# Second attention of a fused layer: scores from three bf16 parts packed by DMA, rotation partner by DMA, batches unrolled and overlapped

## The chip, the cores and the metric

The kernel runs on one core of a Trainium2 chip. The metric is the device time of one execution in microseconds (us). The engines are TensorE (PE; its weight loads are listed as PEld), VectorE (DVE), ScalarE (ACT), GpSimd (POOL) and SyncE (SP), which issues DMAs.

## The reference

A layer over x of 8 batches x 256 positions x 512 features: a first attention whose output feeds the second, the second attention (below), a GRU over the 256 positions and a mixture of 8 experts with top 2. Only the second attention is touched:

```python
q, k, v = (proj(Wq), proj(Wk), proj(Wv))          # 16 heads of 32
q, k = _rope(q, k, s, d, hidden_states.dtype)     # q*cos + rotate_half(q)*sin
scores = jnp.einsum('bhqd,bhkd->bhqk', q, k) / math.sqrt(d)
scores = jnp.maximum(scores + causal, neg)
tmp_attn = jax.nn.softmax(scores.astype(jnp.float32), axis=-1)
tmp_sum = jnp.sum(tmp_attn, axis=-2)
_, topk_idx = jax.lax.top_k(tmp_sum, heavy_budget)       # 25 of 256 columns
heavy_mask = jnp.any(topk_idx[..., :, None] == jnp.arange(s), axis=-2)
band = jnp.abs(i - j) <= recent_budget
scores = jnp.where(heavy_mask[:, :, None, :] | band, scores, neg)
probs = jax.nn.softmax(scores.astype(jnp.float32), axis=-1)
attn = jnp.einsum('bhqk,bhkd->bhqd', probs, v)
return attn @ Wo.T
```

The choice of the 25 columns must come out as in fp32, which is why scores are made in fp32 or from parts that add up to it.

## The kernel before

`program` runs the first attention (its output hT stands in SBUF by 45 us), then `second_attention`, then the GRU and the experts together, which take the rest. Every engine has a program of its own; they are ordered by semaphores alone, and each engine does its instructions in the order written.

`second_attention` goes over the 8 batches in a hardware loop (`Fori`), one batch after another, with two rounds over 16 heads in each. The 512 features are four tiles (KD) of 128, a tile is four heads of 32 rows.

- Projections (`project`, L479) for the next batch: q and k transposed, fp32, 32 matmuls of 256 columns into banks 0 to 3. They run between the rounds, while VectorE chooses columns. ScalarE copies them to `raw` (L612).
- Rotation: `swap` (L490) brings each row's partner with a permutation matmul from the table; VectorE multiplies by sine (L688), by cosine (L691) and adds (L693), 1024 columns each, for q and then k, at the end of a batch. k is then copied four times with the rows of the other heads at zero (`kz`, ScalarE L619 and VectorE L697), so that a score matmul can contract over all 128 rows.
- Round one, `scores(b, 0, h)`: two bf16 matmuls put the causal mask in a bank (L460, L461), then fp32 scores, 128 query rows x 128 columns (L469) and 128 x 256 (L471). Bank is h % 4, so head h waits for the exponentials of head h - 4 (`a_e`). VectorE takes two maxima (L669, L670), ScalarE exponentials with sums (L602, L604), VectorE the reciprocals (L676) into `rdiag` (L707), and for four heads at a time TensorE sums columns (L516). A `v` projection (L505, 8 matmuls of 512 columns, from the copy `hb` that GpSimd makes, L428) precedes the last sums.
- VectorE chooses the 25 largest columns for the 16 heads at once (L717 to L733), TensorE transposes the result (L526), VectorE copies it (L736), GpSimd makes a diagonal matrix for each head (L421).
- Round two, `scores(b, 1, h)`: as before with three more bf16 matmuls by the diagonals (L466 to L468); then normalised (L747, L749), transposed three heads behind (L544), copied (L638), attended in fours (L560, L563), copied to `oT` (L643, L645). At the batch's end the output projection (L575) into banks 0 to 3, and VectorE adds it to `x1T` (L757). The next batch's first score waits for the first add (`v_x`).

Of the kernel before, what the change touches and what calls it, by code (L numbers as in the profile page):

```python
# [13 lines left out]
P = 128  # L14
# [27 lines left out]
C_ROT = 0  # L42
C_CAUS = C_ROT + P
# [312 lines left out]
def second_attention(nc, ps, cst, ident, x1T, hT, tab, weights, d_w, d_tab, d_xT, sb, sem):  # L356
    st = ExitStack()
    with st:
        wq, wk, wv, wo = weights
        masks = sb(st, "masks", [P, 4, P], BF16)  # L360
        hb = sb(st, "hb", [P, KD, S])
        raw = sb(st, "raw", [P, 2, KD, S])
        rot = sb(st, "rot", [P, 2, KD, S])
        kz = sb(st, "kz", [P, HPC, KD, S])
        v = sb(st, "v", [P, KS, D])
        tmp = sb(st, "tmp", [P, KD, S])
# [18 lines left out]
        c_hb = sem(st, "c_hb")  # L385
        p_qk = sem(st, "p_qk")
        a_raw = sem(st, "a_raw")
        p_rot = sem(st, "p_rot")
        v_rot = sem(st, "v_rot")
        a_kz = sem(st, "a_kz")  # L390
        v_kz = sem(st, "v_kz")
# [19 lines left out]

        with nc.Block() as block:
            @block.gpsimd
            def _(pool):
                def diagonals(b):

                    pool.wait_ge(v_l, b + 1)
                    for h in range(NH):
                        if h >= NDG:
                            pool.wait_ge(p_s, b * 2 * NH + NH + h - NDG + 2)  # L420
# [5 lines left out]
                with pool.Fori(0, B) as b:  # L426
                    pool.wait_ge(p_v, b + 1)
                    nc.gpsimd.tensor_copy(hb[:, :, :], hT[:, :, bass.ds(b, 1), :].rearrange("p k a s -> p k (a s)"))\  # L428
                        .then_inc(c_hb, 1)
                    diagonals(b)  # L430

            @block.tensor
            def _(pe):

                pe.nop().then_inc(p_v, 1)
                pe.nop().then_inc(p_s, 1)
# [4 lines left out]
                def scores(b, r, h, more=False):  # L441
# [4 lines left out]
                    if r == 0 and h < 4:  # L446
                        if h == 0:
                            pe.wait_ge(v_x, b * KD + 1)
                    else:
                        pe.wait_ge(a_e, (n - 4 + 1) * 2)  # L450
                    if r == 0 and h == 0:
                        pe.wait_ge(v_rot, b * 6 + 6)
                    if r == 0 and h < 2:
                        pe.wait_ge(a_kz, b * 2 + h + 2)
                    elif r == 0 and h < HPC:
                        pe.wait_ge(v_kz, b * 2 + h - 1)
                    if r == 1 and h == 0 and more:
                        pe.wait_ge(a_raw, b * 2 + 4)
# [3 lines left out]
                    if r == 1:  # L462
# [11 lines left out]
                def project(b):  # L474

                    for i, w in enumerate((wq, wk)):
                        for m in range(KD):
                            for k in range(KD):
                                last = nc.tensor.matmul(ps[:, 2 * i + m // 2, (m % 2) * S:(m % 2 + 1) * S],  # L479
                                                        w[:, k, m * P:(m + 1) * P],  # L480
                                                        hT[:, k, bass.ds(b, 1), :].rearrange("p a s -> p (a s)"),
                                                        start=(k == 0 and m % 2 == 0), stop=(k == KD - 1),
                                                        skip_group_check=True)
                        last.then_inc(p_qk, 1)

                def swap(b, i):

                    pe.wait_ge(a_raw, b * 2 + i + 1)
                    for m in range(KD):
                        last = nc.tensor.matmul(ps[:, 4 + 2 * i + m // 2, (m % 2) * S:(m % 2 + 1) * S],  # L490
                                                tab[:, C_ROT:C_ROT + P], raw[:, i, m, :],
                                                start=(m % 2 == 0), stop=True, skip_group_check=True)
                    last.then_inc(p_rot, 1)

                def batch(b, more):

                    for h in range(NH + AHEAD_SUMS):
                        if h < NH:
                            scores(b, 0, h)
                        if h == NH:  # L500

                            pe.wait_ge(c_hb, b + 1)
                            for c in range(KS):
                                for k in range(KD):
                                    last = nc.tensor.matmul(ps[:, 6 + c, :], hb[:, k, c * P:(c + 1) * P], wv[:, k, :],  # L505
                                                            start=(k == 0), stop=(k == KD - 1))
                            last.then_inc(p_v, 1)
                        g = h - AHEAD_SUMS
                        if g >= 0 and g % CGS == CGS - 1:

                            g0 = g - CGS + 1
# [18 lines left out]
                    for h in range(NH + AHEAD + 1):  # L530
                        if h < NH:
                            scores(b, 1, h, more)
# [1108 lines left out]
```

## Time and profile before

| | us |
|---|---|
| median of 3 runs (lowest to highest) | 2241.44 (2241.01 to 2247.59) |
| the profiled execution | 2239.64 |
| its span, first to last instruction | 2237.8 |
| mean granted TensorE clock | 0.947 |
| busy PE / PEld / DVE / ACT / POOL | 2033.8 / 1748.2 / 1325.7 / 950.0 / 230.7 |

A line of the page's table of slices is a share of busy time in tenths for 40 slices of 56 us; the second attention is slices 1 to 13. A timeline row is start, duration, engine, line, operation, output<-input, shape and count; what stands in brackets is the idle time before it and what ended it. PE durations include the pipeline, so that what a matmul costs is read from start to start.

### The profile page before, as it was taken

How to read it: one execution, taken by the hardware profiler on the slowest of the kernel's cores; microseconds unless marked ns; L12 is line 12 of the kernel's file. 1: busy time of each engine (PE TensorE's matmuls, PEld its weight loads, DVE VectorE, ACT ScalarE, POOL GpSimd, SP SyncE). 2: the span in 40 equal slices, each digit the busy share in tenths (PEclk: the TensorE clock that was granted, in tenths of full speed). 3: DMA queues.
4: the chain of work that ended last, by engine and by line, in shares of the span. 5: the costliest groups of instructions: out<-in, count | busy, mean ns of one | idle time of the engine just before them, and what ended most of it. 6: DMA issues, size and time to landing. Idle time of an engine off the chain costs nothing.

```text
span 2237.8 us, 86088 instructions
## 1 busy us (share of the span) xinstructions
PE 2033.8 (91%) x34733; PEld 1748.2 (78%) x34733; DVE 1325.7 (59%) x4942; ACT 950.0 (42%) x3354; POOL 230.7 (10%) x346
## 2 busy tenths in 40 slices
PE   5889999999996889766999999998999989999999
PEld 3677677767665768666898998898998988988987
DVE  3565575575565079555666666665666656666653
ACT  1355364464453212233444444443444444444432
POOL 0011011011102100000011010110110110111012
PEclk9999999999997999865899999999999999999999
DMA  6000000000000832200000000000000000000000
GB/s 249 1 1 0 0 0 0 0 0 0 0 1 32 291 113 73 67 17 3 18 17 18 13 18 18 27 4 19 27 4 28 18 19 13 18 18 13 4 12 10
DMA packets 53629, 66.07 MB, mean 30 GB/s; under 512 B 4384, under 2 KB 45792, under 8 KB 52416
## 3 DMA queue, kind: packets, MB, share of 16 engines
q1 hardware_dynamic: 50832, 46.48, 6.2%
q0 software_dynamic: 2448, 14.68, 2.0%
q8 instruction: 250, 4.10, 0.8%
q14 instruction: 99, 0.81, 0.1%
HBM read 44.34 MB, written 16.81 MB: 27 GB/s over the span
## 4 chain that ended last, share of the span: by engine, by line
PE 51%; DVE 4%; issue 2%; ACT 1%; DMA 0%; DVEq 0%; POOL 0%; ACTq 0%
PE ps L1302 27%; PE ps L1256 11%; PE ps L1236 11%; PE ps L1290 2%; PE ps L1245 1%; DVE hbuf L1472 1%; DVE dh L1460 0%; DVE dh L1466 0%; DVE hbuf L1469 0%; DVE cn L1450 0%; DVE ns L1462 0%; DVE h L1470 0%; ACT nn L1369 0%; DVE s L1438 0%; DVE cn L1438 0%
## 5 line engine op out<-in xcount | busy, mean ns | idle before, releaser
L1302 PE MATMUL ps<-hbuf,whf 128*128 128x32 f16 x24480 | 659.1, 178 | 82.9 <-DVE hbuf L1472 59.9
L1302 PEld LDWEIGHTS ps<-hbuf,whf 128*128 128x128 f16 x24480 | 648.3, 97 | 106.0 <-DVE hbuf L1472 60.4
L1349 ACT ACTIVATE rz<-s,sc 128x32 f32<-128x32 f32 x512 | 164.5, 321 | 524.1 <-DVE s L1438 512.6
L1236 PE MATMUL ps<-hbuf,w1f 128*128 128x256 f16 x2304 | 294.4, 275 | 0.0
L1256 PE MATMUL ps<-hh,w2f 128*128 128x256 f16 x2304 | 294.1, 276 | 0.0
L1438 DVE TENSOR_REDUCE s<-ps 128x32 f32<-128x64 f32 x512 | 114.5, 224 | 272.7 <-PE ps L1302 259.4
L1425 POOL TENSOR_TENSOR hh<-tb,hh 128x256 f16<-128x256 f32 x192 | 132.3, 694 | 1307.2 <-ACT hh L1396 1307.2
L1236 PEld LDWEIGHTS ps<-hbuf,w1f 128*128 128x128 f16 x2304 | 224.5, 98 | 33.3 <-issue 6.0
L1256 PEld LDWEIGHTS ps<-hh,w2f 128*128 128x128 f16 x2304 | 212.0, 98 | 45.9 <-issue 19.6
L946 PE MATMUL ps<-x1T,wi 128*128 x768 | 173.7, 389 | 21.2 <-DMA wi<-in_W_ih 12.6
L946 PEld LDWEIGHTS ps<-x1T,wi 128*128 128x128 f32 x768 | 149.1, 195 | 45.4 <-issue 19.6
L471 PE MATMUL ps<-kz,rot 128*128 128x256 f32 x512 | 160.2, 396 | 0.0
L1341 ACT ACTIVATE ps<-gi,sc 128x64 f32<-128x64 f32 x512 | 152.7, 298 | 13.8 <-issue 9.9
L1438 DVE TENSOR_REDUCE cn<-ps 128x32 f32<-128x64 f32 x256 | 57.4, 224 | 138.5 <-PE ps L1302 138.5
L421 POOL TENSOR_TENSOR dg<-masks,lcol 128x256 bf16<-128x256 bf16 x128 | 78.2, 616 | 568.7 <-DVE lcol L736 490.9
L602 ACT ACTIVATE E<-ps,nm 128x128 f32<-128x128 f32 x256 | 94.2, 368 | 85.9 <-DVE nm L670 83.0
L1386 ACT ACTIVATE sg<-ps,b,sc 128x256 f32<-128x256 f32 x192 | 105.1, 548 | 48.1 <-PE ps L1236 48.1
L604 ACT ACTIVATE E<-ps,nm 128x256 f32<-128x256 f32 x256 | 119.9, 468 | 0.0
L1534 DVE SCALAR_TENSOR_TENSOR tb<-ps,b1s,sg 128x256 f32<-128x256 f32 x192 | 92.1, 480 | 43.5 <-ACT sg L1386 42.2
L469 PE MATMUL ps<-kz,rot 128*128 128x128 f32 x512 | 117.6, 313 | 0.0
L972 ACT ACTIVATE stage<-ps,bsum 128x256 f32<-128x256 f32 x96 | 44.8, 473 | 167.0 <-PE ps L946 141.0
L669 DVE TENSOR_REDUCE nm<-ps 128x1 f32<-128x128 f32 x256 | 73.7, 288 | 55.6 <-PE ps L471 55.2
(198 smaller groups left out, 2876.3 us busy)
## 6 DMA issues: line engine op xcount, KB each, us to landing
gi_d<-stage SPq DMA_DIRECT2D x96, 128.0 KB, 1.7
gi<-gi_d SPq DMA_DIRECT2D x16, 768.0 KB, 5.5
w1f<-in_w1T POOLq DMA_DIRECT2D x4, 1408.0 KB, 9.2
xall<-in_x SPq DMA_DIRECT2D x4, 1024.0 KB, 9.0
x1T<-in_xT SPq DMA_DIRECT2D x1, 4096.0 KB, 21.7
w2f<-in_w2T POOLq DMA_DIRECT2D x2, 2048.0 KB, 11.0
out<-x1T SPq DMA_DIRECT2D x8, 512.0 KB, 3.1
wi<-in_W_ih SPq DMA_DIRECT2D x1, 3072.0 KB, 10.5
```

The source lines that it names most:

```text
L469: nc.tensor.matmul(ps[:, bank, 0:P], rot[:, 0, m, 0:P], kz[:, q, m, 0:P], start=False, stop=True, skip_group_check=True)
L471: nc.tensor.matmul(ps[:, bank, P:P + S], rot[:, 0, m, P:S], kz[:, q, m, :], start=False, stop=True, skip_group_check=True).then_inc(p_s, 1)
L604: nc.scalar.activation(E[:, h % NEX, P:P + S], ps[:, bank, P:P + S], ACT.Exp, bias=nm[:, r, h, 1:2], accum_out=ls[:, r, h, 1:2]).then_inc( ...
L946: last = nc.tensor.matmul(ps[:, q % 4, 0:TT], wi[:, k, q * P:(q + 1) * P], x1T[:, k, bass.ds(t * SPT, SPT), :].rearrange("p s b -> p (s b) ...
L1236: last = nc.tensor.matmul(ps[:, 6 + i % 2, 0:TT], w[:, wp, e % EH, c * P:(c + 1) * P], hbuf[par][:, k, hq, :, :].rearrange("p s b -> p (s ...
L1256: last = nc.tensor.matmul(ps[:, 4 + m // 2, (m % 2) * TT:(m % 2 + 1) * TT], w[:, wp, e % EH, m * P:(m + 1) * P], hh[:, i % RING, hq, :], s ...
L1302: last = nc.tensor.matmul(ps[:, bank, g * WIDE * 2 * B:(g + 1) * WIDE * 2 * B], whp[:, k, w, q, g * P:(g + 1) * P], h[:, k, :, :].unsqueez ...
L1341: return nc.scalar.activation(of_bank(bank), of.unsqueeze(2).broadcast_to((P, KD, 2, B)), ACT.Copy, scale=sc[:, S_G2:S_G2 + 1])
L1349: nc.scalar.activation(rz[:, q, :, :].rearrange("p g b -> p (g b)"), s1[:, q, :, :].rearrange("p g b -> p (g b)"), ACT.Sigmoid, scale=sc[: ...
L1386: nc.scalar.activation(sg[:, i % 2, :], ps[:, 6 + i % 2, 0:TT], ACT.Sigmoid, bias=b1[:, c, e:e + 1], scale=sc[:, S_UN1:S_UN1 + 1]).then_in ...
L1425: nc.gpsimd.tensor_tensor(hh[:, i % RING, 1, :], tb[:, i % TB, :], hh[:, i % RING, 0, :], ALU.subtract).then_inc(g_l, 1)
L1438: nc.vector.tensor_reduce(o, of_bank(bank).rearrange("p g a b -> p g b a"), AX.X, ALU.add)\
```

## The change

All of it is in `second_attention` and its table.

1. Scores. After rotation, GpSimd splits q and k into three bf16 parts (`split`: high part, remainder, middle part, low part; four operations on 512 columns for each of four units). SP stores the parts to DRAM (`store`) and loads them back (`pack`), for each head three parts under one another on 96 partitions, in two "ways" (`SLOTS`). A score is then two accumulating bf16 matmuls in place of one fp32, giving the six products that matter. `kz` and its copies go.
2. The rotation partner: eight DMAs from SBUF to SBUF for each unit, each 16 partitions x 2 KB, take the place of the permutation matmuls.
3. A unit is q or k for two of the four feature tiles (`UNITS`). Projection (8 parts), raw copies (4), rotation (12 steps of 512 columns) for the next batch stand in round one at given heads, as does the rest of the batch before (last three transposes, last attend, output projection, adds).
4. The values are projected from hT directly in two halves around the last column sums; `hb` goes. Batches are unrolled in Python; there are four diagonals in flight instead of three.

Core of the diff (the first "for b in range(B)" is SP's program, the second TensorE's, the third VectorE's round one):

```diff
+NU = 4
+UNITS = ((0, 0), (1, 0), (0, 1), (1, 1))
+UNIT_BANK = (6, 6, 7, 6)
+PROJECT_AT = (0, 1, 3, 4, 6, 7, 8, 10)
+RAW_AT = (2, 5, 8, 11)
+ROTATE_AT = (4, 5, 6, 7, 8, 9, 10, 11, 12, 13, 14, 15)
+CLOSE_AT = (12, 13)
+ADD_AT = (14, 15)
+SLOTS = (((0, 0, 1), (1, 0, 2)), ((0, 1, 0), (1, 2, 0)))
+            @block.sync
+                def swap(b, u):
+                    i, p = UNITS[u]
+                    sp.wait_ge(a_raw, b * NU + u + 1)
+                    passed(sp, v_rot, (b * NU + u - 1) * 3)
+                    half = DH2 // 2
+                    for to in range(0, P, half):
+                        of = to + half if to % DH2 == 0 else to - half
+                        sp.dma_start(swp[to:to + half, u % 2, :, :], raw[of:of + half, i, 2 * p:2 * p + 2, :])\
+                            .then_inc(d_swap[u % 2], 16)
+                def store(b, u):
+                    sp.wait_ge(g_part, (b * NU + u + 1) * 4)
...
+                    for j in range(3):
+                        sp.dma_start(parts_d[i, j][:, p * 2 * S:(p + 1) * 2 * S],
+                                     parts[:, i, j, 2 * p:2 * p + 2, :].rearrange("p m s -> p (m s)"))\
+                            .then_inc(d_parts[u], 16)
+                def pack(b, p):
+                    for u in (2 * p, 2 * p + 1):
+                        sp.wait_ge(d_parts[u], (b + 1) * 3 * 16)
+                    if b:
+                        sp.wait_ge(p_s, b * 2 * NH - NH + (p + 1) * NH // 2)
+                    for i in range(2):
+                        for way in range(2):
+                            for slot, j in enumerate(SLOTS[i][way]):
+                                of = parts_d[i, j].rearrange("(q d) n -> d q n", d=DH2)
+                                sp.dma_start(pk[slot * DH2:(slot + 1) * DH2, i, way, :, 2 * p:2 * p + 2, :]
+                                             .rearrange("d q m s -> d q (m s)"),
+                                             of[:, :, p * 2 * S:(p + 1) * 2 * S]).then_inc(d_pack[p], 16)
+                for b in range(B):
+                    swap(b, 0)
+                    swap(b, 1)
+                    store(b, 0)
+                    swap(b, 2)
+                    store(b, 1)
+                    swap(b, 3)
+                    store(b, 2)
+                    store(b, 3)
+                    for p in range(2):
+                        pack(b, p)
+                def split(b, u):
...
+                    x = raw[:, i, 2 * p:2 * p + 2, :]
...
+                    nc.gpsimd.tensor_copy(part[0], x).then_inc(g_part, 1)
+                    nc.gpsimd.tensor_tensor(x, x, part[0], ALU.subtract).then_inc(g_part, 1)
+                    nc.gpsimd.tensor_copy(part[1], x).then_inc(g_part, 1)
+                    nc.gpsimd.tensor_tensor(part[2], x, part[1], ALU.subtract).then_inc(g_part, 1)
+                    if r == 0 and h % (NH // 2) == 0:
+                        pe.wait_ge(d_pack[h // (NH // 2)], (b + 1) * PACK)
-                    nc.tensor.matmul(ps[:, bank, 0:P], rot[:, 0, m, 0:P], kz[:, q, m, 0:P],
-                                     start=False, stop=True, skip_group_check=True)
-                    nc.tensor.matmul(ps[:, bank, P:P + S], rot[:, 0, m, P:S], kz[:, q, m, :],
-                                     start=False, stop=True, skip_group_check=True).then_inc(p_s, 1)
+                    for way in range(2):
+                        nc.tensor.matmul(ps[:, bank, 0:P], pk[:, 0, way, q, m, 0:P], pk[:, 1, way, q, m, 0:P],
+                                         start=False, stop=(way == 1), skip_group_check=True)
+                    for way in range(2):
+                        last = nc.tensor.matmul(ps[:, bank, P:P + S], pk[:, 0, way, q, m, P:S],
+                                                pk[:, 1, way, q, m, :],
+                                                start=False, stop=(way == 1), skip_group_check=True)
...
+                for b in range(B):
+                    for h in range(NH):
+                        scores(b, 0, h)
+                        if b and h < AHEAD:
+                            turn(b - 1, NH - AHEAD + h)
+                        if b and h == AHEAD:
+                            attend(b - 1, KD - 1)
+                        if b < B - 1 and h in PROJECT_AT:
+                            u, part = divmod(PROJECT_AT.index(h), 2)
+                            if part == 0:
+                                if u == 0:
+                                    passed(pe, a_o, (b - 1) * KD + KD - 1)
...
+                                if u % 2 == 1:
+                                    pe.wait_ge(a_raw, (b + 1) * NU + u // 2 + 1)
+                            project(b + 1, u, part, UNIT_BANK[u])
+                        if b and h in CLOSE_AT:
+                            m = CLOSE_AT.index(h)
+                            close(b - 1, m, 5)
+                        if h >= AHEAD_SUMS and (h - AHEAD_SUMS) % CGS == CGS - 1:
...
+                            column_sums(b, (h - AHEAD_SUMS) // CGS)
...
+                    values(b, 0)
+                    column_sums(b, NH // CGS - 1)
+                    values(b, 1)
+                    if b:
+                        pe.wait_ge(v_x, (b - 1) * KD + 2)
+                        close(b - 1, 2, 5)
+                        close(b - 1, 3, 5)
...
+                def rotate(b, u, step):
...
+                    x, y = raw[:, i, 2 * p:2 * p + 2, :], swp[:, u % 2, :, :]
...
+                    if step == 0:
+                        dve.wait_ge(d_swap[u % 2], (b * 2 + u // 2 + 1) * 8 * 16)
+                        nc.vector.tensor_tensor(y, y, sin, ALU.mult).then_inc(v_rot, 1)
+                    if step == 1:
+                        nc.vector.tensor_tensor(x, x, cos, ALU.mult).then_inc(v_rot, 1)
+                    if step == 2:
+                        dve.wait_ge(v_rot, n + 2)
+                        nc.vector.tensor_tensor(x, x, y, ALU.add).then_inc(v_rot, 1)
...
+                for b in range(B):
+                    for h in range(NH):
+                        maxima(b, 0, h)
...
+                            for_sums(b, h - 1)
+                        if b < B - 1 and h in ROTATE_AT:
+                            u, step = divmod(ROTATE_AT.index(h), 3)
+                            rotate(b + 1, u, step)
+                        if b and h in ADD_AT:
...
+                            add(b - 1, ADD_AT.index(h), 5)
-NDG = 3
+NDG = 4
```

ScalarE's program for round one is: `exps(b, 0, h)`, at heads 0 and 1 the last two copies of transposes of the batch before, at head 4 its last `oT` copy, and after the exponentials of heads 2, 5, 8 and 11 a raw copy of 512 columns. In round two VectorE adds the last two parts of the batch before at heads 0 and 1.

## Rows read from the trace of the kernel before

**Rows 1.** One row each of the source views of L717 and L757, all batches.

```profile
L717 DVE COPY tsum<-ps x8: 424/424/425, 100.7 to 670.4; 128x256 f32<-128x256 f32 x8
...
L757 DVE TENSOR_TENSOR x1T<-ps,x1T x32: 595/612/629, 154.5 to 719.4; 128x256 f32 x28, 128x256 f32<-128x256 f32 x4
```

**Rows 2.** Windows: length, busy PE, PEld, DVE, ACT, POOL, then PEclk, DMA share, GB/s.

```profile
197.46:225.35 27.89, 25.68 (x257) 20.64 (x257) 20.43 (x80) 21.36 (x83) 10.62 (x17) 1.00 0.00 0
...
74.36:79.60 5.24, 5.24 (x21) 4.14 (x22) 1.92 (x9) 2.81 (x9) 0.00 (x0) 0.50 0.00 0
```

**Rows 3.** Timeline: start, us, engine, line; TensorE, a head of round one.

```profile
244.45 0.22 PE L460 MATMUL ps<-masks 128*128 128x128 bf16 x1
...
244.56 0.44 PE L469 MATMUL ps<-kz,rot 128*128 128x128 f32 x2
244.83 0.60 PE L471 MATMUL ps<-kz,rot 128*128 128x256 f32 x2
245.27 0.22 PE L460 MATMUL ps<-masks 128*128 128x128 bf16 x1
```

**Rows 4.** Timeline: VectorE, a head of round two.

```profile
205.77 0.28 DVE L669 TENSOR_REDUCE nm<-ps 128x1 f32<-128x128 f32 x1
...
205.97 0.41 DVE L670 TENSOR_REDUCE nm<-ps 128x1 f32<-128x256 f32 x1
...
207.09 0.28 DVE L669 TENSOR_REDUCE nm<-ps 128x1 f32<-128x128 f32 x1
```

**Rows 5.** Timeline: ScalarE, a head of round two.

```profile
206.41 0.37 ACT L602 ACTIVATE E<-ps,nm 128x128 f32<-128x128 f32 x1
...
207.22 0.49 ACT L638 ACTIVATE ET<-ps 128x384 f32<-128x384 f32 x1
```

**Rows 6.** Timeline: TensorE and VectorE in the middle of a batch.

```profile
174.52 7.03 PE L505 MATMUL ps<-wv,hb 128*128 128x512 f32 x16
181.48 0.86 PE L516 MATMUL ps<-E,rdiag 128*32 128x128 f32 x16
...
196.18 0.61 PE L526 MATMUL ps<-cst,light 128*128 128x128 f32 x4
...
196.83 0.42 DVE L736 COPY lcol<-ps 128x256 f32<-128x256 f32 x1 [7.73 <-PE ps L526]
...
198.00 0.23 PE L466 MATMUL ps<-dg,masks 128*128 128x128 bf16 x1 [0.26 <-POOL dg L421]
```

**Rows 7.** Timeline: TensorE at the tail of a batch.

```profile
228.91 7.07 PE L575 MATMUL ps<-oT,wo 128*128 128x256 f32 x32
238.66 0.23 PE L460 MATMUL ps<-masks 128*128 128x128 bf16 x1 [2.69 <-DVE x1T L757]
```

**Rows 8.** Timeline: DMA issues of SyncE.

```profile
8.06 0.32 SPq L145 DMA_DIRECT2D scr_bias<-bias  x1
8.42 0.31 SPq L146 DMA_DIRECT2D scr_ksc<-ksc  x1
...
729.19 1.29 SPq L925 DMA_DIRECT2D b<-in_b1T  x3
```

**Rows 9.** DMA view: issues, KB each, median us to landing.

```profile
bgi<-in_b_ih SPq DMA_DIRECT2D x1, 6.0 KB, 1.7
```

**Rows 10.** Groups by line in 0 to 800 us: busy us, mean ns.

```profile
L688 DVE TENSOR_TENSOR tmp<-ps,tab 128x1024 f32<-128x1024 f32 x16 | 19.6, 1225 | 50.8 <-PE ps L490 31.5 <-issue 18.4
...
L421 POOL TENSOR_TENSOR dg<-masks,lcol 128x256 bf16<-128x256 bf16 x128 | 78.2, 616 | 568.7 <-DVE lcol L736 490.9 <-PE ps L471 77.6
```

**Rows 11.** Timeline: a GpSimd copy and a VectorE multiply beside it.

```profile
216.56 1.04 POOL L428 COPY hb<-hT 128x1024 f32 x1
...
216.78 0.89 DVE L747 TENSOR_SCALAR En<-E,rl 128x128 f32<-128x128 f32 x1
```

**Rows 12.** Timeline: TensorE at the first score, and the last output projection.

```profile
74.36 0.29 PE L460 MATMUL ps<-masks 128*128 128x128 bf16 x1 [6.88 <-ACT kz L619]
...
709.92 9.46 PE L575 MATMUL ps<-oT,wo 128*128 128x256 f32 x32 [0.53 <-ACT oT L645]
```

More of the change, by code:

```diff
@@ L424, in diagonals @@
                             .then_inc(g_d, 1)
[L426 to L429, printed above, removed]
+                for u in range(NU):
+                    split(0, u)
+                for b in range(B):
+                    if b < B - 1:
+                        for u in range(NU):
+                            split(b + 1, u)
                     diagonals(b)
@@ L486, in swap @@
[L486 to L511, printed above, removed]
-                            pe.wait_ge(v_d, b * NH + g + 1)
-                            for part, (e0, e1) in enumerate(((0, P), (P, P + S))):
-                                for g in range(g0, g0 + CGS):
-                                    rows = (g % CGS) * CG
-                                    last = nc.tensor.matmul(ps[rows:rows + CG, 4, 0:e1 - e0], rdiag[:, g, part, :],
-                                                            E[:, g % NEX, e0:e1], start=(g0 == 0 and part == 0),
-                                                            stop=(g0 + CGS == NH and part == 1),
-                                                            tile_position=(0, rows), skip_group_check=True)
-                            last.then_inc(p_c, 1)
-                    if more:
-                        pe.wait_ge(a_e, (b * 2 * NH + NH) * 2)
-                        project(b + 1)
-                    pe.wait_ge(v_k, b * K_STEPS + K_STEPS)
@@ new lines, in scores, with project @@
+                    last.then_inc(p_s, 1)
+                def project(b, u, part, bank):
+                    i, p = UNITS[u]
+                    w = (wq, wk)[i]
+                    m = 2 * p + part
+                    for k in range(KD):
+                        last = nc.tensor.matmul(ps[:, bank, part * S:(part + 1) * S], w[:, k, m * P:(m + 1) * P],
+                                                hT[:, k, b, :], start=(k == 0 and part == 0), stop=(k == KD - 1),
+                                                skip_group_check=True)
+                    if part == 1:
+                        last.then_inc(p_qk, 1)
@@ new lines, in close @@
+                def close(b, m, bank):
+                    pe.wait_ge(a_o, (b + 1) * KD)
+                    o = ps[:, bank, (m % 2) * S:(m % 2 + 1) * S]
+                    for k in range(KD):
+                        last = nc.tensor.matmul(o, wo[:, k, m * P:(m + 1) * P], oT[:, k, :],
+                                                start=(k == 0 and m % 2 == 0), stop=(k == KD - 1),
+                                                skip_group_check=True)
+                    last.then_inc(p_o, 1)
@@ L579, in _ @@
-                project(0)
-                for i in range(2):
-                    swap(0, i)
-                with pe.Fori(0, B - 1) as b:
-                    batch(b, True)
-                batch(B - 1, False)
+                            attend(b, g // HPC)
+                for g in range(NH - AHEAD, NH):
+                    turn(B - 1, g)
+                attend(B - 1, KD - 1)
+                for m in range(KD):
+                    close(B - 1, m, 2 * (m // 2))
             @block.scalar
@@ L652, in _ @@
+                for g in range(NH - 2, NH):
+                    turned(B - 1, g)
+                attended(B - 1, KD - 1)
             @block.vector
```

346 lines of the change are left out of this document (168 added, 178 removed).

## Prediction, made before the changed kernel was run

> **What bounds the kernel now.** I read the source view first, to bound the part that is changed: the eight column sums are copied out at a pitch of (670.4 - 100.7) / 7 = 81.4 us, so this is a batch's period, and the last add to x1T starts at 719.4 and ends at 720.0 [rows 1]. The second attention is thus 720.0 - 45 of the 2237.8 us; nothing behind it is touched. Then the timeline of one batch, where the reader looks for who is late at each step:
> - Round one, 17.5 us: a head costs TensorE 0.11 for two mask matmuls, 0.27 for fp32 scores on 128 columns and 0.44 on 256 columns, 0.82 in all [rows 3].
> - The middle: values 174.52 to 181.48, column sums 0.8, projections of the next batch until 196.18, then the transpose of the chosen columns, and the first diagonal matmul of round two at 198.00 [rows 6]. VectorE had its choice ready at 196.83 - 7.73 = 189.1: it waits for TensorE.
> - Round two, 27.9 us to the end of the last attend: TensorE is busy for 25.68, but DVE for 20.43 and ACT for 21.36 too [rows 2], and both run without a gap at 1.32 a head [rows 4, 5]. Three engines are nearly level, so a cheaper TensorE frees little here.
> - The tail: swap matmuls, the output projection from 228.91, 7.07, rotation and x1T adds on DVE, until TensorE resumes at 238.66 after 2.69 idle [rows 7].
>
> **The change part by part.** I cost a period of the new loop in three stretches, each by the engine that ends it.
>
> *Scores.* Four bf16 matmuls take the place of the two fp32. Masks at 0.057 for 128 columns [rows 3] are the nearest rows; 2 x 0.057 + 2 x 0.115 = 0.34 against 0.71, so 0.37 off a head. If K=96 tiles with fresh weights load slower, the bound is no gain. Round two's TensorE head falls from 1.32 to 0.95, and DVE with ACT become its bound.
>
> *Round two, from its first diagonal matmul.* First maxima 1.1 later, maxima 0.6, fifteen further heads at 1.30 (I take 1.30 of the 1.32 [rows 4], as POOL and TensorE get out of the way little), two adds of 0.6 moved into it [rows 1], and then ACT: exponentials of head 15 at 0.81 [rows 5], one turned copy 0.49, one oT copy 0.38 and a release. 1.1 + 0.6 + 19.5 + 1.2 + 1.9 = 24.3. There the next batch's first projection part may start, since it waits on that oT copy. The pack DMAs of heads 0 to 7 are issued at head 7: 12 issues at 0.45 and 1.7 to land, some 7 to 10 us with 1.5 MB to move, against 11 us or more; cost zero, hidden by the second half of round two, and up to 5 if that cover is gone.
>
> *Round one.* TensorE's work from here: 15 scores x 0.46 = 6.9, eight projection parts x 1.77 = 14.1 (16 matmuls took 7.07 [rows 7]), two output parts 3.5, three column sums 2.4, turns and one attend 1.5: 28.3, and the first half of the values 3.5: 31.8 until the last column sums. DVE's work is smaller (about 23). But the rotation partner is now a transfer in the middle of DVE's program. Four times DVE reaches the multiply by sine (heads 4, 7, 10, 13) and waits for eight DMAs, and the maxima of all later heads are queued behind that wait; ACT's exponentials, and behind them the next raw copy, wait for those maxima. The loop from the end of one such multiply to the next wait's end is:
> - DVE maxima of the next head 0.62, release 0.07;
> - ACT exponentials 0.81 [rows 5] and raw copy of 512 columns 0.6 (0.49 for 384 [rows 5]): 1.41, release 0.1;
> - SP: eight issues. Two DMAs of 8 rows x 2 KB started 0.36 apart [rows 8]; three others took 0.43 each [rows 8]. I take 0.38, so the last starts 2.66 after the first;
> - landing 1.7 [rows 9], plus 0.1.
>
> That is 6.7, plus the multiply on 512 columns, 0.65 (1225 for 1024 [rows 10]): 7.3 for three heads, where DVE's own work would be 4.5 and TensorE's 5.4. Bounds on the swap itself: 3.5 to 6.
>
> *POOL and DVE.* A split is two copies and two two-input operations: 2 x 0.55 (1.04 for 1024 columns [rows 11]) + 2 x 1.2 (616 ns for 256 [rows 10]) + waits = 3.9. It begins after the third rotation step, so it ends about when the next partner lands. A DVE instruction that met a POOL copy took 0.89 where its like took 0.29 [rows 11]: I add 0.5 for each of three units, between 0 and 1.2. The Trainium skill (SBUF — State Buffer, Who interferes with whom) says that a DVE operation with two SBUF inputs is shut out for the whole of a GpSimd instruction that reads SBUF; with a full 1.2 for each unit the time would be 2230, an estimate by that page. The row shows only the one-input form, and agrees that far.
>
> So round one: first swap landed at 11.6 after the start of the first projection part (4.3 of projections and scores, 2.8 of maxima, exponentials and copy, 4.5 of swap), 0.65, three loops 3 x (7.3 + 0.5) = 23.4, then heads 14 and 15 with steps and adds 4.8: 40.5. TensorE's 31.8 is hidden below it. The Trainium skill (DMA: Bandwidth & Descriptors, Anatomy of one DMA) gives about 2.0 us fixed for a DMA, where [rows 9] show 1.7; by the page's figure, an estimate, the time would be 2223.
>
> *Middle.* Column sums 0.8; then values' second half and two output parts, 3.5 + 3.5 = 7.1, against DVE's choice of 189.1 - 181.5 = 7.6 with the sums in it: level. But TensorE has by then sat idle for some 5 us. After 6.88 idle [rows 12] its granted clock was 0.50, the 1.2 GHz level, for 5.24 us [rows 2], and one output projection took 9.46 [rows 12] where the other took 7.07 [rows 7]; 2.4 more, between 0 and 4. Transpose at 196.18 to diagonal matmul at 198.00: 1.8 [rows 6]. Sum 12.1.
>
> *Period:* 24.3 + 40.5 + 12.1 = 76.9 against 81.4.
>
> *Start.* Before, the first score starts at 74.36 [rows 12]. Now SP's queue serialises the start: unit 0 is projected at about 53.6, copied, swapped, rotated and split by 65; the swap of unit 2 stands on SP behind the store of unit 0, that of unit 3 behind the store of unit 1, and the packs behind the last store. 65 + store 1.3 + swap of unit 2 and store of unit 1 5 + swap of unit 3 4.5 + rotation 2 + split 3.9 + store 1.3 + pack 8 = 91: 17 later.
>
> *Last batch* has no projections and no swap: DVE 16.5 to the sums, middle 9.7, round two 24.3, then three copies and the last attend 3.1, output projection 9.46 cold and an add 0.6: 63.7. In the first batch round one is 2.9 longer: a first score of 0.5, and 2.4 for the clock of a start after idle.
>
> *End* = 91 + 79.8 + 6 x 76.9 + 63.7 = 695.9, against 720.0: 24 us sooner. The profiled execution took 2239.6 with a span of 2237.8; 2239.6 - 24 = 2215. Its median of runs is 2 us higher, which is inside the error.
>
> **The rivals.**
> - *The partner lands in time.* If the swap takes under 2.8 us or DVE gets ahead, round one ends with TensorE at 31.8, TensorE is never idle (middle 9.7), the period is 65.8: seven times 11.1 less, 2137. For it: each transfer is only 32 KB. Against: eight issues of 0.36 by rows of this trace are 2.5 before any landing. 0.20.
> - *POOL's split is long, and slower than before.* SP stores unit 0 before it may swap unit 2, and unit 1 before unit 3. With a split of 3.9 the store is done about 1 us before the swap could be issued. If fp32 doubles the price of two-input operations (the row is bf16 alone), a split is 7: two swaps are late by 2.2 each and the rotations meet POOL's lock for 2 more, 6.4 a batch, 2260. It decides from 3.4 a batch, a split of about 5.5. 0.17.
> - *The scores don't get cheaper*: the bf16 matmuls are as slow as fp32. TensorE stays level with DVE in round two and under the swap waits in round one: 1 us a batch, 2222. 0.05.
>
> **How the numbers follow.** Forecast 0.58, its own range 2190 to 2240 (swap 3.5 to 6 would be -28 to +42 for all units, cold clock -17 to +11, seldom together). To leave out 2 in 10 the range takes in the first rival and half of the second: 2135 to 2255. A change of 0.3%, 7 us, is what a measurement can tell. Faster 0.76 (most of forecast, first and third rival), within 0.08, slower 0.16.
>
> **What would show it.** DVE idle before the sine multiply, released by the swap DMA, about 2 to 4 us, four times a batch; period 77; TensorE idle some 5 us before the last column sums and slow scores or values behind it; first score near 91; round two at 1.3 a head with TensorE idle in it; bf16 score matmuls 57 and 115 ns apart. What makes it wrong: a swap much shorter or longer than 4.5, a late pack (TensorE waiting at head 0 for DMA), or TensorE still full in round two.

## The result: slower by 0.6%, and the profile after

The changed kernel takes 2255.64 us (median of 7 runs, 2250.0 to 2261.17) against 2241.44; the ratio is 1.0056, with a 95% interval of 1.0041 to 1.0072. The forecast was 2215, range 2135 to 2255, faster. The direction was wrong. The profiled execution took 2250.0, the shortest of the seven, with a span of 2248.2. Its page (engine busy times; granted clock in 40 slices; waits for DMA do not show here):

```profile
span 2248.2 us, 85076 instructions
...
PE 1935.9 (86%) x34605; PEld 1655.0 (74%) x34605; DVE 1309.5 (58%) x4974; ACT 927.3 (41%) x3362; POOL 336.4 (15%) x466
...
PEclk9689989989989899956899999999999999999999
```

TensorE is busy 98 us less than before and the span is 10.4 us longer. Source views of the copy of the column sums, one a batch, and of the x1T adds, answering [rows 1]:

```profile
L831 DVE COPY tsum<-ps x8: 424/425/426, 145.0 to 690.5; 128x256 f32<-128x256 f32 x8
...
L800 DVE TENSOR_TENSOR x1T<-ps,x1T x32: 606/616/626, 220.7 to 733.3; 128x256 f32<-128x256 f32 x32
```

The last add ends at 733.9 where it ended at 720.0. The pitch, (690.5 - 145.0) / 7 = 77.9, has the short last batch in it; over the six full batches between the first column sums (144.1) and the seventh (634.3) it is 81.7. Four of the longest waits of the stretch with the second attention in it (us in total, times, longest):

```profile
ACT E L688 <- DVE nm L756: 277.6, 101, 35.0
DVE swp L775 <- DMA swp<-raw: 153.2, 32, 12.6
...
PE ps L561 <- DVE rdiag L794: 79.5, 22, 6.3
...
PE ps L518 <- DMA pk<-parts_d: 33.9, 1, 33.9
```

VectorE waits 153 us for `swp<-raw`, four times in each of 8 batches. Batch 1 to 2 in the new kernel, TensorE, from the first projection part to the last column sums, then to the first diagonal matmul, then to the next batch's first projection part:

```profile
177.24 1.99 PE L542 MATMUL ps<-hT,wq 128*128 128x256 f32 x8 [1.28 <-ACT oT L713]
...
212.68 1.51 PE L561 MATMUL ps<-E,rdiag 128*32 128x128 f32 x16 [4.20 <-DVE rdiag L794]
...
223.58 0.86 PE L561 MATMUL ps<-E,rdiag 128*32 128x128 f32 x16 [3.71 <-DVE rdiag L794]
...
233.06 0.61 PE L654 MATMUL ps<-cst,light 128*128 128x128 f32 x4
...
234.88 0.23 PE L524 MATMUL ps<-dg,masks 128*128 128x128 bf16 x1 [1.10 <-POOL dg L489]
...
258.64 1.99 PE L542 MATMUL ps<-hT,wq 128*128 128x256 f32 x8 [1.28 <-ACT oT L713]
```

That is 46.3 + 11.3 + 23.8 = 81.4 a batch. The middle is 5.2 shorter than before (16.5, [rows 6]) and the old tail of 13.3 is gone [rows 2, 7], but all that and more went into round one. TensorE waits 4.20 and 3.71 for VectorE before its last two column sums.

Answering [rows 3] and [rows 4], a bf16 pair of score matmuls in round one and two maxima of successive heads of round two:

```profile
186.33 0.28 PE L528 MATMUL ps<-pk 96*128 96x128 bf16 x2
186.44 0.38 PE L531 MATMUL ps<-pk 96*128 96x256 bf16 x2
...
242.78 0.29 DVE L755 TENSOR_REDUCE nm<-ps 128x1 f32<-128x128 f32 x1
...
243.97 0.28 DVE L755 TENSOR_REDUCE nm<-ps 128x1 f32<-128x128 f32 x1
```

The bf16 scores came as priced: 0.11 us for two of 128 columns. Where nothing holds it, round two runs at 1.19 us a head on VectorE, not 1.32; over the fifteen steps of this round two, from the first maxima at 235.59 to the last at 257.07, it is 1.35 without the two adds. TensorE's saving is real; it ends in waits.

### The profile page after: what moved, and what is told of

Read it like the earlier page. It is cut to its first block, busy times and chain, and to the rows that moved or that the text cites. A ratio compares the mean times of both kernels' runs of the same rounds, so it can differ in the third digit from the quotient of the medians.

```text
span 2248.2 us, 85076 instructions
## 1 busy us (share of the span) xinstructions
PE 1935.9 (86%) x34605; PEld 1655.0 (74%) x34605; DVE 1309.5 (58%) x4974; ACT 927.3 (41%) x3362; POOL 336.4 (15%) x466
## 4 chain that ended last, share of the span: by engine, by line
PE 50%; DVE 4%; issue 2%; ACT 1%; DMA 0%; DVEq 0%; POOL 0%; ACTq 0%
PE ps L1415 27%; PE ps L1369 11%; PE ps L1349 10%; PE ps L1403 2%; PE ps L1358 1%; DVE hbuf L1585 1%; DVE dh L1573 1%; DVE dh L1579 1%; DVE cn L1563 0%; DVE hbuf L1582 0%; ACT nn L1482 0%; DVE h L1583 0%; DVE cn L1551 0%; DVE ns L1575 0%; DVE hn L1566 0%
## 5 line engine op out<-in xcount | busy, mean ns | idle before, releaser
L775 DVE TENSOR_TENSOR swp<-swp,tab 128x512 f32<-128x512 f32 x32 | 22.9, 715 | 153.2 <-DMA swp<-raw 153.2
L756 DVE TENSOR_REDUCE nm<-ps 128x1 f32<-128x256 f32 x256 | 106.0, 414 | 0.0
L531 PE MATMUL ps<-pk 96*128 96x256 bf16 x512 | 103.4, 285 | 0.0
```

The costliest lines, as they stand in the source:

```text
L531: last = nc.tensor.matmul(ps[:, bank, P:P + S], pk[:, 0, way, q, m, P:S], pk[:, 1, way, q, m, :], start=False, stop=(way == 1), skip_group ...
L756: nc.vector.tensor_reduce(nm[:, r, h, 1:2], ps[:, bank, P:P + S], AX.X, ALU.max, negate=True).then_inc(v_m, 1)
```

## The ring in round one

A ring is a chain of waits that closes on itself: here VectorE waits for a transfer, and the next transfer can only be requested after work that stands behind this wait. VectorE's sine multiplies of batch 2's units, with the idle time before each and what ended it, and one turn of the ring from ScalarE's exponentials over the raw copy to SP's eight DMAs:

```profile
190.69 0.69 DVE L775 TENSOR_TENSOR swp<-swp,tab 128x512 f32<-128x512 f32 x1 [2.93 <-DMA swp<-raw]
...
200.73 0.69 DVE L775 TENSOR_TENSOR swp<-swp,tab 128x512 f32<-128x512 f32 x1 [5.74 <-DMA swp<-raw]
...
209.73 0.69 DVE L775 TENSOR_TENSOR swp<-swp,tab 128x512 f32<-128x512 f32 x1 [4.70 <-DMA swp<-raw]
...
218.72 0.69 DVE L775 TENSOR_TENSOR swp<-swp,tab 128x512 f32<-128x512 f32 x1 [4.70 <-DMA swp<-raw]
...
201.99 0.37 ACT L688 ACTIVATE E<-ps,nm 128x128 f32<-128x128 f32 x1 [6.32 <-DVE nm L756]
...
202.80 0.59 ACT L698 ACTIVATE raw<-ps 128x512 f32<-128x512 f32 x1
...
203.41 4.94 SPq L426 DMA_DIRECT2D swp<-raw  x8
```

From 200.73: exponentials start 1.26 later, raw copy 0.81 behind that, its end at 203.39, SP issues from 203.41 for 4.94, and the last of the eight lands 1.38 later, when the next multiply starts at 209.73. 1.26 + 0.81 + 0.59 + 0.02 + 4.94 + 1.38 = 9.0. Eight DMAs of 32 KB take SP 0.62 us each, where the prediction took 0.38 with 0.43 as the dear end of its rows [rows 8].

The turn before it, from 190.69 to 200.73, takes 10.0, and SP's row for its eight DMAs shows where:

```profile
193.37 5.96 SPq L426 DMA_DIRECT2D swp<-raw  x8
```

One of these eight took SP 1.61 where the others took 0.51 to 0.59. In each batch one turn is longer than 9.0 in this way (9.4 to 10.2). Why a single issue is so long now and then stays open.

Theory A: this ring, and in it the number of issues, sets round one. Rivals: the landing or the bytes (B), the order of the engines' programs whatever brings the partner (C), TensorE after all (D), GpSimd's splits, or the unrolled instruction stream (G). All ratios below are to the kernel before.

## Experiments

**One DMA for the partner.** It leaves out the exchange of rows and moves the same bytes; VectorE's wait, not shown in the cut, then counts one DMA.

```diff
-                    for to in range(0, P, half):
-                        of = to + half if to % DH2 == 0 else to - half
-                        sp.dma_start(swp[to:to + half, u % 2, :, :], raw[of:of + half, i, 2 * p:2 * p + 2, :])\
-                            .then_inc(d_swap[u % 2], 16)
+                    sp.dma_start(swp[:, u % 2, :, :], raw[:, i, 2 * p:2 * p + 2, :]).then_inc(d_swap[u % 2], 16)
```

> Leaves out the exchange of rows: the partner is copied by one DMA of 128 partitions x 2 KB in place of eight of 16 partitions, so each unit still crosses the same bytes and the same wait, with one issue. Theory A (the eight issues, 4.94 us on SP in the changed kernel, make the loop of 9.0 us between sine multiplies): the loop shortens by the seven issues of 0.62, 9.0 - 4.3 = 4.7 us, which is near VectorE's own work for three heads, so round one falls to what TensorE needs: a batch shorter by 10 to 14 us, the whole by 75 to 110 us. Rival B (the wait is the landing of a DMA and the lock that GpSimd's split holds, not the count): the loop stays above 8 us and the whole moves by less than 20 us.

Measured 2160.56 us, ratio to before 0.9637 (0.9609 to 0.9665), 95 us below the changed kernel. VectorE's sine multiplies, then SP's single issue:

```profile
173.39 0.68 DVE L771 TENSOR_TENSOR swp<-swp,tab 128x512 f32<-128x512 f32 x1
...
179.49 0.98 DVE L771 TENSOR_TENSOR swp<-swp,tab 128x512 f32<-128x512 f32 x1 [0.67 <-DMA swp<-raw]
...
185.85 0.79 DVE L771 TENSOR_TENSOR swp<-swp,tab 128x512 f32<-128x512 f32 x1 [0.86 <-DMA swp<-raw]
...
177.22 0.47 SPq L423 DMA_DIRECT2D swp<-raw  x1
```

In this batch they are 6.1 to 6.4 apart and the wait is gone or under 1 us; in others single turns take up to 7.6. The ring alone had expected 4.7; by then TensorE is the one without a gap, busy in the whole 6.10 from 173.39 to 179.49. Same bytes, an eighth of the issues: A, against B.

**Four DMAs**, again without the exchange of rows and with VectorE's wait to match:

```diff
-                    for to in range(0, P, half):
-                        of = to + half if to % DH2 == 0 else to - half
-                        sp.dma_start(swp[to:to + half, u % 2, :, :], raw[of:of + half, i, 2 * p:2 * p + 2, :])\
+                    for to in range(0, P, DH2):
+                        sp.dma_start(swp[to:to + DH2, u % 2, :, :], raw[to:to + DH2, i, 2 * p:2 * p + 2, :])\
```

> Leaves out the exchange of rows: the partner is copied by four DMAs of 32 partitions in place of eight of 16, the same bytes. Between the changed kernel (eight, sine multiplies 9.0 us apart) and the run with one DMA (6.1 to 6.4 apart, where VectorE and TensorE set the pace). Theory A, the price is per issue, 0.62 us on SP: 9.0 - 4 x 0.62 = 6.5 us apart, so nearly the whole gain of one DMA: 2170 to 2190 us. Rival B, the price is per byte or per row: four DMAs take SP about as long as eight, and the time stays above 2230 us.

Measured 2189.06 us, ratio 0.9767 (0.9748 to 0.9787). Sine multiplies and SP:

```profile
175.81 0.69 DVE L773 TENSOR_TENSOR swp<-swp,tab 128x512 f32<-128x512 f32 x1 [0.44 <-DMA swp<-raw]
...
182.55 1.35 DVE L773 TENSOR_TENSOR swp<-swp,tab 128x512 f32<-128x512 f32 x1 [1.09 <-DMA swp<-raw]
...
189.93 1.13 DVE L773 TENSOR_TENSOR swp<-swp,tab 128x512 f32<-128x512 f32 x1 [2.43 <-DMA swp<-raw]
...
196.88 1.35 DVE L773 TENSOR_TENSOR swp<-swp,tab 128x512 f32<-128x512 f32 x1 [2.21 <-DMA swp<-raw]
...
193.06 2.41 SPq L424 DMA_DIRECT2D swp<-raw  x4
...
182.20 1.16 POOL L479 TENSOR_TENSOR parts<-raw,parts 128x512 bf16<-128x512 f32 x1
```

Four DMAs of twice the size take SP 2.41, 0.60 each. The price is per issue. The multiplies are 6.7 to 7.4 apart, not 6.5, because three of the four shown take 1.13 to 1.35 instead of 0.69: now that the partner lands earlier, the multiply meets GpSimd's split, the lock that the prediction had put into the slower ring. The multiply at 182.55 starts while the last operation of a split runs, until 183.36, and ends 0.54 behind it. In other batches single turns reach 8.6, where one of SP's four issues took 1.97.

**Two queues, the whole swap.** Partitions 0 to 63 are issued by SP and 64 to 127 by GpSimd, ahead of its splits, with a semaphore of its own (only the new order of GpSimd's program is shown):

```diff
+                def swaps_and_splits(b):
+                    swap(b, 0)
+                    swap(b, 1)
+                    split(b, 0)
+                    swap(b, 2)
+                    split(b, 1)
+                    swap(b, 3)
+                    split(b, 2)
+                    split(b, 3)
```

> The swap is whole again, all eight DMAs, but four are issued by SP and four by GpSimd, ahead of its splits. Theory A (time of one sequencer's issues): the eight overlap in two queues, sine multiplies about 6.5 to 7 us apart, 2185 to 2210 us. Rival B (the DMA engines take that long for eight SBUF to SBUF transfers, whoever issues): they stay 9 us apart and the time near 2255. Rival E: GpSimd's issue is dearer than SP's or is held by VectorE's lock on the shared port, then 8 to 10 us apart with the last landing coming from GpSimd's half.

Measured 2199.89 us, ratio 0.9816 (0.9796 to 0.9835): with all eight transfers in place, 56 us below the changed kernel. SP and GpSimd each issue four; below them, VectorE's sine multiplies:

```profile
192.27 2.42 SPq L427 DMA_DIRECT2D swp<-raw  x4
...
192.54 1.95 POOL L492 DMA_DIRECT2D swp<-raw  x4 [2.81 <-ACT raw L719]
...
181.06 0.69 DVE L797 TENSOR_TENSOR swp<-swp,tab 128x512 f32<-128x512 f32 x1 [1.60 <-DMA swp<-raw]
...
188.69 1.60 DVE L797 TENSOR_TENSOR swp<-swp,tab 128x512 f32<-128x512 f32 x1 [2.06 <-DMA swp<-raw]
...
196.26 0.69 DVE L797 TENSOR_TENSOR swp<-swp,tab 128x512 f32<-128x512 f32 x1 [2.37 <-DMA swp<-raw]
```

They are 7.6 apart here, a little more than the 6.5 to 7 expected, and not 9.0; GpSimd's issues are no dearer than SP's. The same eight transfers land in time for that, so it was not the transfers but one sequencer's issues, one behind the other, that made the ring long.

**The rotation three steps at a time, later.**

```diff
-                        if b < B - 1 and h in ROTATE_AT:
-                            u, step = divmod(ROTATE_AT.index(h), 3)
-                            rotate(b + 1, u, step)
+                        if b < B - 1 and h in (6, 9, 12, 15):
+                            for step in range(3):
+                                rotate(b + 1, (h - 6) // 3, step)
```

> Swap DMAs unchanged; only VectorE's place for the rotation moves: all three steps of a unit at heads 6, 9, 12, 15 instead of one step a head from head 4. The raw copy of the next unit (head 5, 8, 11) then stands ahead of the wait and not behind it. Theory A (it is the ring maxima - exponentials - raw copy - swap - multiply that costs 9.0 us, not the transfers): the ring is cut, the waits overlap with work, round one ends near TensorE's or SP's pace: a batch of 70 to 76 us, the whole 45 to 80 us less. Rival B (the transfers' own rate or GpSimd's split bounds it): less than 20 us.

Measured 2198.06 us, ratio 0.9817 (0.9785 to 0.985), 58 us below the changed kernel and inside what A expected. Not one transfer differs. The wait at head 4 stood ahead of the maxima whose exponentials precede the next raw copy; the wait at head 6 stands behind those of head 5, and the swaps run beside work:

```profile
185.33 0.69 DVE L775 TENSOR_TENSOR swp<-swp,tab 128x512 f32<-128x512 f32 x1
...
192.44 0.69 DVE L775 TENSOR_TENSOR swp<-swp,tab 128x512 f32<-128x512 f32 x1 [0.24 <-DMA swp<-raw]
...
199.06 0.69 DVE L775 TENSOR_TENSOR swp<-swp,tab 128x512 f32<-128x512 f32 x1 [1.86 <-DMA swp<-raw]
...
206.03 0.69 DVE L775 TENSOR_TENSOR swp<-swp,tab 128x512 f32<-128x512 f32 x1 [1.10 <-DMA swp<-raw]
...
191.19 1.46 SPq L435 DMA_DIRECT2D parts_d<-parts  x3
...
192.75 4.94 SPq L426 DMA_DIRECT2D swp<-raw  x8
```

Between the second and the third multiply SP itself sets the pace: its swap issues end at 191.06, three stores and eight more issues follow without a wait, until 197.69, and 6.6 is what they take.

So there are two ways out of the ring: a shorter swap, or a wait that does not hold the next request.

**GpSimd: casts only.**

```diff
-                    nc.gpsimd.tensor_tensor(x, x, part[0], ALU.subtract).then_inc(g_part, 1)
+                    pool.nop().then_inc(g_part, 1)
...
-                    nc.gpsimd.tensor_tensor(part[2], x, part[1], ALU.subtract).then_inc(g_part, 1)
+                    nc.gpsimd.tensor_copy(part[2], x).then_inc(g_part, 1)
```

> The changed kernel with GpSimd's splits cut to three casts, without the two subtractions (the parts are then wrong): 1.8 us of GpSimd a unit in place of 3.7. Theory A: the swap ring holds the pace, the split lies inside the wait for the next partner: sine multiplies still 9.0 us apart, less than 15 us of the whole, and that at the start and through earlier stores. Rival (GpSimd's lock or the stores behind the split are in the ring, which the prediction priced at 0.5 us a unit): 0.5 to 1 us a unit less, 15 to 30 us.

Measured 2248.94 us, ratio 1.0038 (1.0025 to 1.0051), 6.7 us less; 3.5 of that stands at the start, where the first score comes at 93.22 and not at 96.71. The ring is unchanged:

```profile
197.47 0.69 DVE L775 TENSOR_TENSOR swp<-swp,tab 128x512 f32<-128x512 f32 x1 [5.47 <-DMA swp<-raw]
...
206.47 0.69 DVE L775 TENSOR_TENSOR swp<-swp,tab 128x512 f32<-128x512 f32 x1 [4.70 <-DMA swp<-raw]
...
215.48 0.69 DVE L775 TENSOR_TENSOR swp<-swp,tab 128x512 f32<-128x512 f32 x1 [4.71 <-DMA swp<-raw]
```

The 0.5 us a unit that the prediction gave to the lock is not in this ring. In the changed kernel a split runs from 194.25 to 198.00 and the next multiply starts at 200.73: they don't meet.

**Half of the score matmuls** (one of the two ways left out):

```diff
-                    for way in range(2):
+                    for way in range(1, 2):
```

> Leaves out half of the score matmuls (one of the two ways), packs as before. Theory A: TensorE is on nobody's path in either round, so 32 x 0.17 = 5.5 us less of its work a batch changes the whole by less than 8 us. Rival D (TensorE's head still sets round two): 2 to 3 us a batch, 15 to 25 us.

Measured 2251.2 us, ratio 1.0051 (1.0033 to 1.0069), 4.4 us less of the 44 us that the cut takes off TensorE, which is within the spread of the runs (2248.6 to 2256.9 here, 2250.0 to 2261.2 for the changed kernel). D falls for the scores: what they cost TensorE is not on the path.

**The partner by TensorE again.** The permutation matrix is back in the table, and a partner is two fp32 matmuls into bank 5 at heads 4, 7, 10 and 13. SP keeps stores and packs.

```diff
+                def partner(b, u):
+                    i, p = UNITS[u]
+                    n = b * NU + u
+                    pe.wait_ge(a_raw, max(n + 1, 2))
+                    passed(pe, v_rot, (n - 1) * 3 + 1)
+                    if u == 0:
+                        passed(pe, a_t, (b - 1) * NH)
+                    for j in range(2):
+                        last = nc.tensor.matmul(ps[:, 5, j * S:(j + 1) * S], tab[:, C_ROT:C_ROT + P],
+                                                raw[:, i, 2 * p + j, :], start=(j == 0), stop=True,
+                                                skip_group_check=True)
+                    last.then_inc(p_rot, 1)
...
-CLOSE_AT = (12, 13)
+CLOSE_AT = (14, 15)
```

> The partner comes from a permutation matmul again (two fp32 matmuls of 256 columns into bank 5), inside round one; scores, packs, unrolling and overlap stay; the output parts in round one move from heads 12 and 13 to 14 and 15 because they share the bank. Theory A (the swap DMAs are what eats the gain): no DMA wait in VectorE's program, TensorE's 28.3 + 3.6 for the partners + 3.5 bound round one, a batch of 68 to 72 us against 82, first score 10 to 15 us earlier, the whole 85 to 115 us below the changed kernel, and so below the kernel before. Rival C (the overlap itself is too tight: VectorE, ScalarE and TensorE block one another in round one whatever brings the partner): less than 40 us below the changed kernel.

Measured 2187.75 us, ratio 0.9767 (0.9737 to 0.9796): 68 us below the changed kernel and below the kernel before, but between what A (85 to 115) and C (under 40) expected. The first score starts only 3.2 us sooner, at 93.51, because the packs still stand on SP behind the last store. Round one, by the start of its first projection part and of its last column sums:

```profile
162.88 1.99 PE L526 MATMUL ps<-hT,wq 128*128 128x256 f32 x8 [1.27 <-ACT oT L719]
...
190.74 1.13 PE L541 MATMUL ps<-raw,tab 128*128 128x256 f32 x4 [1.26 <-ACT raw L704]
...
193.03 1.99 PE L603 MATMUL ps<-oT,wo 128*128 128x256 f32 x8 [0.72 <-DVE swp L781]
...
201.45 0.86 PE L559 MATMUL ps<-E,rdiag 128*32 128x128 f32 x16
```

38.6 us, against 46.3 with the swap and 35.4 reckoned: TensorE waits 1.26 for the raw copy of the last unit and 0.72 for VectorE, and is busy in 36.05 of it.

**The same with the first pack early.** For batch 0, pack of heads 0 to 7 ahead of the stores of units 2 and 3:

```diff
-                    for u in range(NU):
-                        store(b, u)
+                    for p in range(2):
+                        store(b, 2 * p)
+                        store(b, 2 * p + 1)
+                        if b == 0:
+                            pack(b, p)
...
+                    if b:
+                        for p in range(2):
+                            pack(b, p)
```

> The kernel with the partner by permutation matmul, and for batch 0 alone the pack of heads 0 to 7 moved ahead of the stores of units 2 and 3 on SP. Theory F (the start is serial on SP: packs behind the last store, first score at 93.5 us): the first score comes 6 to 9 us sooner and the whole 5 to 9 us, 2179 to 2183 us. Rival: the second pack is then late for head 8 and nothing is won.

Measured 2176.43 us, ratio 0.9717 (0.9694 to 0.9739), the fastest kernel here that leaves nothing out, 79 us below the changed kernel and 2.8% below the one before. The first score starts at 88.09, 5.4 sooner:

```profile
88.09 0.29 PE L506 MATMUL ps<-masks 128*128 128x128 bf16 x1 [15.79 <-DMA pk<-parts_d]
```

That is a little less than the 6 to 9 expected. The median fell by 11.3, more than the 5 to 9 expected, but the two medians are of 4 runs each and the earlier kernel's runs spread over 13 us. The profiled executions took 2177.12 before this change and 2177.83 with it; in them the second attention ends 2.8 sooner, and what follows it is 3.4 longer. So the gain at the start is shown, its worth for the whole isn't.

**That kernel with half of its score matmuls** (the edit of the run with half of the score matmuls above):

> The kernel with the partner by matmul and the early pack, less half of its score matmuls (one of the two ways left out). In the changed kernel the same cut moved 4.4 us. Theory A: with the swap ring gone TensorE is the bound of round one (15 or 16 heads x 0.17 = 2.7 us a batch), not of round two: 12 to 22 us less than 2176. Rival C (VectorE and the order of the programs bound round one too): less than 8 us.

Measured 2174.49 us (2 runs), ratio 0.9701 (0.9668 to 0.9734): 1.9 less, and in the profiled executions the second attention ends 6.2 sooner. The expectation for A was wrong: even without the ring, TensorE's work on scores hardly sets either round; in the batch after the first, round one is 38.7 with the cut and 38.6 without it, round two 23.8 in both. That is what rival C expected, but C itself, the order of three programs with four banks between them, isn't shown. One sum speaks against it: round one took 34.9 in the run with one DMA, and with the 3.6 of the partner matmuls that makes 38.5.

**The kernel before, unrolled**, and nothing else (TensorE's loop is shown; those of GpSimd, ScalarE and VectorE are changed alike):

```diff
-                with pe.Fori(0, B - 1) as b:
+                for b in range(B - 1):
                     batch(b, True)
```

> The kernel before with its batch loops written out in Python, nothing else. Theory A: unrolling itself is worth nothing or little, the register work of the loop lies beside waits: within 8 us of the kernel before. Rival G: the longer instruction stream costs fetches, the kernel gets slower by 5 to 20 us, and this is a part of why the changed kernel is slower.

Measured 2231.57 us (9 runs), ratio 0.9952 (0.9939 to 0.9965). It is 9 us faster, where nothing or a loss was expected. G falls, and the prediction had this part of the change at nothing. The pitch of its column-sum copies is (663.8 - 100.9) / 7 = 80.4 against 81.4 [rows 1]:

```profile
L717 DVE COPY tsum<-ps x8: 424/425/425, 100.9 to 663.8; 128x256 f32<-128x256 f32 x8
```

## Why the prediction was wrong

- *What ends which stretch*: right. Round one ends by the ring over VectorE, ScalarE and SP, TensorE's work is hidden under it, TensorE idles before the last sums. In round two of the batch read above VectorE has no wait over 0.3 us between the first maxima and the last. The mechanism of the forecast is the mechanism of the result.
- *The step that failed* is the size of one term: the swap, from the end of the raw copy to the landing, at 4.5 (eight issues 0.38 apart, 1.7 to land, 0.1). It took 6.3: 4.94 for the issues and 1.38 behind them. In the prediction's own terms, the last issue starts 4.35 after the first and not 2.66, and lands 1.94 after its start and not 1.7: nearly all of the error is the price of an issue. The ring without the lock was reckoned at 7.3 and took 9.0, once in a batch 9.4 to 10.2. The two rows it rested on were DMAs of 8 rows x 2 KB to DRAM, the dearer row, 0.43, was for loads into up to 128 partitions; neither was SBUF to SBUF. The bound of the whole swap, 6, was below the truth.
- *GpSimd's lock* in the ring, 0.5 for each of three units: nothing. The two mistakes had opposite signs: 3 x 7.8 = 23.4 was forecast for three turns and 28.0 measured.
- *First swap*: 13.45 us after the first projection part (177.24 to 190.69) against 11.6, for the same reason. Round one 46.3 against 40.5.
- *Middle* 11.3 against 12.1, with TensorE at a granted clock of 0.85 in it after 3.71 idle; *round two* 23.8 against 24.3 (23.6 to 24.6 over the batches): both right.
- *Start*: 96.7 against 91. The last swap, reckoned to have landed at 75.8, released VectorE at 80.4, 4.6 late, again by SP's issues; the packs took 9.1 and not 8.
- *The end*, by the last column sums: the first batch's came 9.7 late (144.1 against 134.4), the next six batches 4.8 each, 28.8; the last batch's sums 2.4 more, and from there to the end 2.9 less. 38.0 in all, 733.9 against 695.9. Behind it the remaining 1514.3 us were 3.5 shorter than before; no run changes that part, and in the twelve profiles it took 1513.2 to 1521.7, so the 3.5 is spread and not an effect. 38.0 - 3.5 = 34.5 is the distance from 2215 to the profiled 2250.0; the median is 5.6 above that one.
- *The sum of the bounds*: the text priced a swap of 6 at 42 us, which is 2257 and slower, and still set the range at 2255 and the chance of slower at 0.16, as if the dear end were improbable. Break-even was 3.4 us a batch, 0.9 a swap, and no row of a transfer like this one excluded that. The slower rival named GpSimd's split; the split took 3.75 from its start to its end, against 3.9 reckoned, and ended before the next multiply. That the time fell near this rival's 2260 is luck, its mechanism isn't what happened.
- *The first rival* (partner in time, 2137) is nearest to the run with one DMA, 2160.56. It had round one at TensorE's 31.8 and a batch at 65.8; they took 34.9 and 69.9 there. The first score came at 87.89, where the rivals shared the forecast's 91.
- *Unrolling* was priced at nothing and is worth 9 us alone in the kernel before; in the changed kernel no run has it apart.

Open: why a single issue of SP takes 1 us more once in a batch, and what sets round one at 38.6 when TensorE makes the partner.

## What to carry to other kernels

When a transfer is put in the middle of an in-order engine's program, draw the ring: what the engine holds back while it waits, and whether the next transfer's request is in it. The price of a turn is then the work between, the landing, and the number of issues times the sequencer's time for one (0.62, 0.60 and 0.47 here for 32, 64 and 256 KB); move the wait behind the next request, or cut the number of issues, before anything else. A cheaper instruction on an engine that isn't the one waited for gives next to nothing (44 us of score matmuls less gave 4.4). And when a term of the sum rests on rows of another kind of transfer, its range has to take in the break-even.

## What the runs showed of the hardware

- An SBUF to SBUF DMA of 16 partitions x 2 KB cost SP 0.62 us to issue, one of 32 partitions 0.60, one of all 128 alone 0.47, a store of 128 partitions x 1 KB 0.50; GpSimd issued the 16-partition form in 0.49. Eight small ones take eight times one, with 1.4 us more until the last has landed. From its own issue a 16-partition one landed in 1.9 (median of 256), the one of 128 partitions in 2.3. The 2.0 that the prediction takes from the Trainium skill (DMA: Bandwidth & Descriptors, Anatomy of one DMA) stands there for DMAs that GpSimd issues; SP's 1.9 is near it.
- In each of the seven rings of the changed kernel at least one issue took SP 0.96 to 1.76 us instead of 0.59; why, no run shows.
- A VectorE multiply with both inputs in SBUF took 1.35 and 1.13 instead of 0.69 where it met a GpSimd split. The prediction had that row only for the one-input form. The Trainium skill (SBUF — State Buffer, Who interferes with whom) says that a VectorE instruction with two SBUF inputs contends with a GpSimd instruction that reads SBUF; this trace agrees, with 1.35 against 0.69.
- The Trainium skill (DMA: Bandwidth & Descriptors, Issuing engines are not separate DMA queues) says that issuing from several engines saves only sequencer time, usually small beside the transfer. The first half agrees; here that time was 4.94 of a 9.0 us ring, and two queues gave 56 us.
